# Sixteen small products in diagonal order: one PE loop of a pooling kernel for 2048 candidates

## The reference

```
outer = einsum('bi,bnj->bnij', candidate_ad, goods).reshape(Bs, Ns, Ks * Ks)
k_b = broadcast_to(candidate_ad[:, None, :], (Bs, Ns, Ks))
h1 = concatenate((k_b, goods, outer), axis=-1)
act = sigmoid(h1 @ W1 + b1)
weight = act @ W2 + b2
out = sum(goods * weight, axis=1)
```

## Time and profile before

| | |
|---|---|
| median of 3 runs | 317.15 us (316.57 to 317.31) |
| the profiled execution | 316.4 us |
| its span (first to last instruction) | 314.3 us |
| PE / PEld busy | 292.5 us (93%) / 165.6 us (53%) |
| ACT / DVE / POOL busy | 220.2 us (70%) / 203.6 us (65%) / 183.2 us (58%) |
| mean granted clock of TensorE | 0.968 of full speed |
| the 64 rounds | from 33.5 us to about 301.7 us, nearly all of them 4.12 us long |

### The profile page before, as it was taken

One profiled execution on the slowest core, in us unless ns is written; L12 is line 12 of the kernel. 1 busy time (PEld: TensorE's weight loads), 2 busy tenths in 40 slices (PEclk: granted clock), 3 DMA queues, 4 the chain that ended last, 5 costly groups with the idle time before them and its releaser, 6 DMA issues.

```text
span 314.3 us, 17422 instructions
## 1 busy us (share of the span) xinstructions
PE 292.5 (93%) x7480; PEld 165.6 (53%) x7480; DVE 203.6 (65%) x1114; ACT 220.2 (70%) x602; POOL 183.2 (58%) x261
## 2 busy tenths in 40 slices
PE   2993699999999999999999999999999999999973
PEld 0210255556665566555565555566556655566641
DVE  0999205666666667666666666666666776666676
ACT  0999767777777776777677766777777776777730
POOL 9400035666666666666566665666666666666663
PEclk9997569999999999999999999999999999999997
DMA  7990000666666666656666665666565665663000
GB/s 286 417 374 2 2 2 16 203 207 216 213 200 194 196 186 206 209 198 217 214 207 187 194 179 197 215 214 208 185 195 194 198 208 203 213 211 108 5 3 8
DMA packets 10588, 55.69 MB, mean 177 GB/s; under 512 B 1168, under 2 KB 1936, under 8 KB 10384
## 3 DMA queue, kind: packets, MB, share of 16 engines
q1 hardware_dynamic: 10080, 54.01, 52.0%
q10 hardware_dynamic: 432, 0.58, 0.5%
HBM read 54.32 MB, written 0.26 MB: 174 GB/s over the span
## 4 chain that ended last, share of the span: by engine, by line
PE 85%; ACT 9%; DMA 2%; DVE 2%; issue 1%; POOL 0%; POOLq 0%; ACTq 0%; DVEq 0%
PE z_ps L206 26%; PE w_ps L242 24%; PE s_ps L255 21%; PE x_ps L222 14%; ACT wm L286 5%; ACT wx L293 3%; DMA act<-w_outer 2%; DVE goods L345 1%; ACT act L303 1%; PE z_ps L176 1%; ACT L303 0%; ACT L286 0%; POOL mid L160 0%; DVE whole L338 0%; POOLq L40 0%
## 5 line engine op out<-in xcount | busy, mean ns | idle before, releaser
L303 ACT ACTIVATE act<-z_ps,bias 128x200 f32<-128x200 f32 x512 | 169.7, 442 | 67.6 <-PE z_ps L206 67.6
L345 DVE CUSTOM_DVE_ANT_0 goods<-s_ps,goods 128x200 f32<-128x200 f32 x512 | 160.8, 362 | 86.5 <-PE s_ps L255 79.0
L156 POOL TENSOR_SCALAR top<-whole,consts 128x200 bf16<-128x200 f32 x64 | 50.1, 782 | 108.7 <-DVE whole L338 108.7
L206 PE MATMUL z_ps<-goods,wm 32*32 32x200 f32 x4096 | 87.4, 345 | 7.6 <-ACT wx L293 6.9
L255 PE MATMUL s_ps<-stack,pick_sb 128*128 128x200 bf16 x512 | 75.7, 253 | 4.6 <-DVE out_stage L345 3.6
L206 PEld LDWEIGHTS z_ps<-goods,wm 32*32 32x32 f32 x4096 | 50.4, 104 | 30.8 <-issue 12.3
L255 PEld LDWEIGHTS s_ps<-stack,pick_sb 128*128 128x128 bf16 x512 | 32.9, 97 | 58.0 <-issue 38.9
L222 PE MATMUL x_ps<-goods,wx 128*32 128x200 f32 x1024 | 58.6, 340 | 0.0
L242 PE MATMUL w_ps<-act,consts 128*32 128x200 f32 x1024 | 57.8, 342 | 0.0
L160 POOL TENSOR_SCALAR mid<-rest,consts 128x200 bf16<-128x200 f32 x64 | 50.1, 782 | 6.3
L345 DVE DVE_READ_ACCUMULATOR2_ANT out_stage<- 128x1 f32 x512 | 42.6, 83 | 0.0
(11 more groups left out here) (26 smaller groups left out, 73.2 us busy)
## 6 DMA issues: line engine op xcount, KB each, us to landing
goods<-goods_t SPq DMA_DIRECT2D x64, 800.0 KB, 4.3
act<-cand_r SPq DMA_DIRECT2D x1, 1024.0 KB, 5.2
act<-cand_u SPq DMA_DIRECT2D x1, 256.0 KB, 6.0
pick_sb<-pick ACTq DMA_DIRECT2D x1, 256.0 KB, 8.3
out_t<-out_stage SPq DMA_DIRECT2D x4, 64.0 KB, 4.1
consts<-small ACTq DMA_DIRECT2D x1, 164.5 KB, 6.1
act<-w_outer ACTq DMA_DIRECT2D x1, 144.0 KB, 5.4
```

The source lines that it names most:

```text
L156: nc.gpsimd.tensor_scalar(top[:, :], whole[:, q % 2, :], m1, None, ALU.mult).then_inc(part_step, 1)
L206: last = nc.tensor.matmul(z_ps[32 * c:32 * c + 32, r, N * s:N * s + N], wm[32 * r:32 * r + 32, PAIR_U * p + 4 * s + c, :], goods[32 * r:32 ...
L303: last = nc.scalar.activation(act[:, p % A_SLOTS, r, N * s:N * s + N], z_ps[:, r, N * s:N * s + N], ACT.Sigmoid, bias=bias[:, r, p, s:s + 1])
L345: last = nc.vector.tensor_tensor_reduce(goods[:, q % G_SLOTS, v, :], s_ps[f % 2][:, N * i:N * i + N], goods[:, q % G_SLOTS, v, :], 1.0, 0. ...
```

## The change

The 16 products of a half are issued along the diagonals of the array, and no longer row group by row group. For k = 0 to 3 and r = 0 to 3 the product of row group r and column group (r + k) mod 4 is issued. Two things move with it. The wait for `act_done`, which stood ahead of each row group of the first half (for the emptying of bank r alone), is now one wait ahead of all, for the emptying of all four banks. And `z_done` of bank r rises with the product (r, (r + 3) mod 4) of the second half, which is one of the last four of the round, where it rose after the fourth, eighth, twelfth and sixteenth product of that half.

```diff
                 for s in range(2):
-                    for r in range(4):
-                        if s == 0 and p >= 1:
-
-                            pe.wait_ge(act_done, 4 * (p - 1) + r + 1)
-                        for c in range(4):
+                    if s == 0 and p >= 1:
+
+                        pe.wait_ge(act_done, 4 * p)
+                    for k in range(4):
+
+                        for r in range(4):
+                            c = (r + k) % 4
                             last = nc.tensor.matmul(z_ps[32 * c:32 * c + 32, r, N * s:N * s + N],
                                                     wm[32 * r:32 * r + 32, PAIR_U * p + 4 * s + c, :],
                                                     goods[32 * r:32 * r + 32, p % G_SLOTS, 4 * s + c, :],
                                                     start=True, stop=True)
-                        if s == 1:
-                            last.then_inc(z_done, 1)
+                            if s == 1 and k == 3:
+                                last.then_inc(z_done, 1)
```

## The result

The changed kernel takes 322.34 us, the median of 4 runs (320.27 to 322.55), against 316.86 us for the kernel before on the same chip (4 runs, 315.02 to 317.31). The ratio is 1.0168, with a 95% interval of 1.0138 to 1.0198: slower by 5.3 to 5.5 us where 2.2 were forecast. The forecast was 319.3 us in a range of 317.0 to 321.0, so the measured time lies above the range. The sign is right and the size is off.

What follows compares the result with a forecast made beforehand. It took normal rounds as bound by the loop through DVE, with the change making ACT's loop the longest. 317.15 us + 1.5 (later rounds, after credit) + 0.7 (rounds 1 to 4) = 319.3 us; range 317.0 to 321.0.

Steps and rivals of the forecast that it cites:

- The DVE loop of 4.115 us, with `products` under its cover: Normal rounds: spread and DVE close the loop; PE's 0.13 us wait for DVE covers products, so faster products gain nothing.
- The order, 0: In products: issuing along diagonals instead of by row group changes nothing by itself, 0 us, bounded by 0.15 either way.
- `z_done` of bank 0, +0.15: Second half of products: rises with the 29th product, not the 20th, so ACT starts 0.15 us later, 1.36 after products.
- A separate wait answers in 0.15, a wait on the load in 0.05: Ahead of products: release to PE's start takes 0.15 us with its own wait instruction, 0.05 with it on the load.
- The ACT loop 0.04 over the round: Normal rounds: 1.36 + 2.65 + 0.15 = 4.16 us against 4.12, so 0.04 us more in each of 59 steps, 2.4 us.
- credit for the stops: Rounds 4 to 63: the 5 stops in issue hide some of ACT's lateness, 0.85 us off, leaving 1.5 us.
- Rounds 1 to 4, +0.7: Cold start, where PE really waits for ACT: all 16 products start together after the wait, costing 0.7 us.
- D: Rival, chance 0.05: the wait at 37.5 to 39.4 us keeps the clock at 1.2 GHz past 44.75, +6 us, 323 us.
- "After each of the 5 stops in issue, `products` is back on its old place; that step is free.": Rounds after PE's stops ahead of products_x (5, 1.7 us in all): that step costs nothing, next 0.13 us of lateness hides.
- Rival B: Chance 0.06: faster, as PE's stops in issue shrink; half of them gone with the start-up hidden, 316.2 us.

Runs made afterwards that it cites:

- e5: Kernel before with DVE's copy of the row sums moved behind the fourth pair of units: 309.54 us, ratio 0.9781 to the kernel before.
- e1: Changed kernel with the four per-bank act_done waits given back, on the first four products: ratio 1.0002 to the kernel before.
- e2: Kernel before, its order and z_done kept, with only the four act_done waits made one for all banks: 320.72 us, ratio 1.0148.
- e7: Kernel before with only the four z_done rises moved to the last four products of the round: ratio 0.9996.
- e4: Changed kernel with products row group by row group again, keeping the one wait and late z_done: ratio 1.0183 to the kernel before.
- e3: Changed kernel with the wait for the next round's goods moved ahead of products_x, leaving act_done's wait on the load: 320.04 us, ratio 1.0115.
- e11: Changed kernel run once more, unaltered, for a second profile: ratio 1.0172 to the kernel before.
- e10: Changed kernel with two act_done waits: bank 0 ahead of the first product, all four banks on the second product's load; ratio 1.0040 to the kernel before.
- e6: Changed kernel with DVE's copy of the row sums moved behind the fourth pair of units: 319.85 us, ratio 1.0106 to the kernel before.
- e9: e1 with the wait for the next round's goods moved ahead of products_x: ratio 1.0131 to the kernel before.

## Why the prediction was too low

- *The DVE loop of 4.115 us, with `products` under its cover.* Right. It was released by one moved copy (e5), and e1, e2 and e7 keep their round of 4.116.
- *The order, 0.* Right as far as the runs can tell (e4 against the changed kernel; e1).
- *`z_done` of bank 0, +0.15.* Nearly: ACT starts 1.35 us after the first matmul, 1.36 predicted. The two starts in the prediction, 156.77 and 156.91, are 0.14 apart and not 0.15. e7 shows that it costs nothing by itself while ACT has slack.
- *A separate wait answers in 0.15, a wait on the load in 0.05.* Right: 0.14 to the matmul (0.11 to the load). In e3 the same wait on the load gives a normal round of 4.115.
- *The ACT loop 0.04 over the round.* The mechanism was right. 0.027 to 0.032 us measured, 1.6 to 1.9 us over 59 rounds, where the prediction has 2.4 before its credit for the stops and 1.5 after it. That the 1.5 is near is in part luck: the loop was put 0.01 us too long, and the credit did not come.
- *Rounds 1 to 4, +0.7.* 0.7 by the two profiles first compared, 0.9 by the means of two each. Two more rounds at the low clock (D) did not come. The granted clock goes from 0.50 to 1.00 at 44.7 and 45.5 us in the two profiles of the kernel before, and at 45.5 and 46.5 in those of the changed one, so a part of the 0.9 may be the later rise in e11, whose rounds 0 to 3 are the longest of all.
- *"After each of the 5 stops in issue, `products` is back on its old place; that step is free."* This is the step that failed. I took the stops as given, a property of the program's length, 1.7 us whatever the kernel does, and even booked them as a credit of 0.85 us. (The 1.7 are only those ahead of `products_x`; with those in `row_sums` the same profile has 2.6.) They went from 2.6 and 1.3 us in the two profiles of before to 5.3 and 4.0: +2.7 us. With this term the sum closes: 0.9 + 1.8 + 2.7 = 5.4 us by the means of two profiles, against 5.3 to 5.5 measured. Rival B had the right object (the stops can change) with the wrong sign, and I argued it away with "nothing touches the number of instructions". The number is indeed the same, 15,157 in every kernel here; what changed is where PE is held.

In part the larger stops are more of the same kind (longer ones in `row_sums`, late fetches), in part new ones inside `products` that have nothing to hide under once ACT closes the round. In e2, where the DVE loop still covers 0.13 us, a piece of those is hidden.

**What stays open.** That the stops are PE's own instruction fetches is shown by the common place modulo 256 and by the 2.4 us. That the separate late wait brings more of them is shown by e1 and e10 against the changed kernel, and by e2, which has nothing else; e6 has it too and has few, so its size does not carry over from one kernel to the next. Why it does is not. The separate wait ahead of `products` ends 1.15 us before the first load in the kernel before, e1, e7 and e10, 0.16 us before it in e2, and 0.03 us before it in the changed kernel, e4 and e6 (medians over the rounds from 4 on). A sequencer that can't run ahead behind a wait that is not met would ask for the next instructions later; this fits the changed kernel, e2 and e10, but not e9, where no separate wait is left at that place and the fetches are late all the same. Why the stops inside `products` come though their fetch was not late is open too, and so is what is left in e10, 0.4%. Padding the program, which would move the boundaries, was not tried.

## What to carry over

When several fine waits are folded into one, look at how the one is issued: as an instruction of its own at the head of a block it answers up to 0.1 us later than on a load, and here it brought 2.7 us more of instruction stops in a program of 59 fetches (0.9 us in e6 against e5). If it can be had, keep an early-met wait in the separate slot and put the late one on the next instruction (e10). And treat small "issue" gaps as something that a change can make larger, with a range of its own; before one works on the order inside a covered piece, release the loop that covers it, which was one moved line here and worth 2.2%.

## What the runs showed of the hardware

- PE's instructions come in blocks of 256 (16 KB). A block asked for too late stops PE, until 2.2 to 2.6 us after its transfer began (one of 2.8). Single stops are 0.1 to 1.1 us long, and together they are 1.1 to 6.3 us of some 250 in the fourteen profiles, with the same number of instructions in all of them.
- A wait as an instruction of its own ahead of a float32 product: 0.11 us from the releasing sigmoid's end to the load and 0.14 to the matmul. With the wait on the load: 0.05 to the load.
- Loads of 32 x 32 float32 into a row group of the array whose earlier product is in flight follow at the same 7 ns as loads into another row group, and the two orders take the same time (1.0183 with an interval of 1.0148 to 1.0218 in e4, 1.0168 with 1.0138 to 1.0198 in the changed kernel).
